# Moving V's projection ahead of the second half's queries and keys in a transformer layer on one core

## The chip, the cores and the metric

One core of a Trainium2 chip. The time is device microseconds (us) of one execution. Three runs of the kernel before gave 2120.45, 2121.21 and 2126.31 us; the median is 2121.21.

## The reference, cut to what matters

One layer of a transformer with layer norm ahead of attention and of a linear map, for 32 batches of 512 tokens with 256 channels, all float32; 16 heads of 16 channels.

```python
x = L0_attn_x                                    # 32 x 512 x 256
y = layernorm(x)
q, k, v = split_heads(y @ qkv_w.T)               # 16 heads x 16
q, k = rotate(q), rotate(k)                      # rotary positions
attn = q @ k.T * 16 ** -0.5 + alibi              # slopes * 8 * min(key - query, 0)
o = softmax(attn) @ v
x = x + o @ proj_w.T + proj_b
x = x + layernorm(x) @ (W + C @ V_r.T).T + b
```

## The kernel before, in words

Each engine's program is written out by hand, as one pass over slots (`FIRST_SLOT` to `END_SLOT`), and every slot has two halves. Slot 16 b + h does the scores of head h of batch b, so a batch is 16 slots or 32 halves; `now` (2 slot + half) counts halves. In this text half k of a batch is the half with now = 32 (b - 1) + k, from 0 to 31, while the scores of batch b - 1 are made; what is prepared in them is for batch b. Engines wait for one another by semaphores alone, and each runs its own instructions in order.

In every half TensorE (`tensor_program`) does, in this order:
- twice a score for the row maxima (`max_scores`, L428, into one of the two banks of `ps_s`) and a transposed score of the head 11 slots earlier (`exp_scores`, L438, into `ps_t`). The score waits until VectorE has read the one two before it in that bank (`max_done`); the first transposed score of a half waits for the exponential of two halves before (`exp_done`), which reads the same half of `ps_t`.
- what the tables at the top set for this half, all of it in the one bank `ps_misc`. The unit is a quarter: 4 matmuls of 32 x 256, which the trace counts as 8. A table entry (-10, (2, 2)) is: begins at half -10 (22 of the batch before), 2 quarters, then 2. `QK` has four chunks for each batch (queries and keys of heads 0 to 7, then of heads 8 to 15; `project_qk`, L396), `V` two pieces, `PROJ` and `FFN` the output maps (`linear`, L409). `XT`, `X2T` (turns), `DEN` (spread of the denominators, L470) and the row maxima (L461) have halves of their own. The first matmul of each waits until another engine has emptied the bank.
- eight matmuls (the trace's 16) of the weighted values of the head 12 slots earlier (`weighted_values`, L451, into `ps_o`). The last of a head raises `pv_done`.

VectorE reads each score with the bias and takes the row maximum (`row_maximum`, L608), adds the bias of the diagonal blocks to the transposed scores (`diagonal_bias`, L618), and at a few halves takes reciprocals of the denominators (`denominators`, L626), divides or adds. ScalarE takes one exponential a half (L794), and empties `ps_misc` where a filling ends (`empty_bank`): `raw` for queries and keys (L774), `v_one` for V (`place_v`, L750), `xt` for turns. It stands in ScalarE's order ahead of the exponential of that half. Every fourth slot, in the second half, it also copies `ps_o` to `o_sb` (L856). Means and squares of the next batches (L726, L731) stand there too. GpSimd turns `raw` (L944, L946) at the slots in `ROTATE`, and makes the high and low parts of queries and keys (L961 to L968). SP issues the DMAs.

`place_v` for batch b >= 2 has a second wait: `v_one` has two buffers, and V of batch b - 2 must have been used, which is `pv_done` at 16 (b - 1). The copy of `o_sb` waits for `pv_done` of its four heads, and half 23's copy waits for this same count:

```python
            def place_v(b, u):
                act.wait_ge(misc_full, full_at["v", b, u])
                if b >= 2:
                    act.wait_ge(pv_done, H * (b - 1))
```

The raw copy of chunk cc (`empty_bank`) waits for `rope_done` at cc, GpSimd's turn of the chunk before, since `raw` is one buffer.

Of the kernel before, what the change touches and what calls it, by code (L numbers as in the profile page):

```python
# [41 lines left out]
T_LAG, PV_LAG = 11, 12  # L42


QK = ((-24, (2, 1, 1)), (-21, (1, 1, 1, 1)), (-10, (2, 2)), (-4, (2, 1, 1)))
V = ((-8, (2, 2)), (-6, (2, 2)))
PROJ = ((66, (2, 2)), (68, (2, 2)))
FFN = ((82, (2, 2)), (84, (2, 2)))
XT, DEN, X2T = (-26, -25), (63, 64), (79, 80)

ROTATE = (-11, -9, -4, -1)
FIRST_SLOT = -21

SOONER = 8
# [57 lines left out]
def layer(nc, x, qkv_w, proj_w, proj_b, slopes, w, wb, v_r, c_r, consts, out):  # L112
    ctx = ExitStack()
    with ctx:
# [180 lines left out]
        def batch_at(slot, begin):  # L295

            b, off = divmod(slot - begin, H)
            return b if off == 0 and 0 <= b < NB else None
# [18 lines left out]
        def due(half, begin, counts=(1,)):  # L317

            for i, count in enumerate(counts):
                b, off = divmod(half - begin - i, 2 * H)  # L320
                if off == 0 and 0 <= b < NB:
                    return b, range(sum(counts[:i]), sum(counts[:i]) + count)
            return None, ()

        def complete_at(half, begin, counts=(1,)):

            b, off = divmod(half - begin - len(counts) + 1, 2 * H)
            return b if off == 0 and 0 <= b < NB else None

        def chunk_complete(half):  # L330

            for c, piece in enumerate(QK):
                b = complete_at(half, *piece)
# [4 lines left out]
        def chunk_rotated(slot):  # L338
            for c, begin in enumerate(ROTATE):
                b = batch_at(slot, begin)  # L340
                if b is not None:
                    return 4 * b + c
            return None
# [5 lines left out]
        def head_at(slot, begin):  # L349
            return slot - begin if 0 <= slot - begin < NH else None  # L350
# [12 lines left out]
        def tensor_program():  # L363
# [142 lines left out]
            for slot in range(FIRST_SLOT, END_SLOT):  # L506
# [9 lines left out]
                for half in range(2):  # L516
# [6 lines left out]
                    for u in range(2):  # L523
                        b, quarters = due(now, *V[u])
                        for quarter in quarters:
# [14 lines left out]
                    for c in range(4):  # L540
                        b, quarters = due(now, *QK[c])
                        for quarter in quarters:
# [19 lines left out]
        def vector_program():  # L562
# [25 lines left out]
            def normalise_last():  # L588

                dve.wait_ge(rstd_done2, NB)  # L590
                dve.nop(nofuse=True)
                for t in range(T):
                    ins = dve.tensor_scalar(x_hat2[:, t, :], x1[:, t, :], minus_mean[:, 1, t:t + 1],  # L593
                                            rstd[:, 1, t:t + 1], ALU.add, ALU.mult)
                ins.then_inc(xhat_done2, 1)

            def row_maximum(n, t):
                hb, hh = divmod(n, 8)
                h, k = n % H, T * n + t
                if hh == 0 and t == 0 and hb >= 2:  # L600
                    dve.wait_ge(max_split, hb - 1)
                if n < H and t == 0:
                    dve.wait_ge(alibi_done, h + 1)
                dve.wait_ge(s_done, k + 1)
                dve.nop(nofuse=True)
                off = FREE + h * N - t * P
                unused = early_junk[:, t, :] if n < T_LAG else junk[:, t % 2, :]
                dve.tensor_tensor_reduce(unused, scores_bank(n, t), alibi[:, off:off + N], 1.0, LOWEST,  # L608
                                         ALU.add, ALU.max, row_max[:, hb % 2, t, hh:hh + 1]).then_inc(max_done, 1)

            def diagonal_bias(n, pair):

                h = n % H
                dve.wait_ge(t_done, T * n + 2 * pair + 2)
                whole = ps_t[:, :, :]
                blocks = bass.AP(whole.tensor, whole.offset + 2 * pair * (N + P), [[T * N, P], [N + P, 2], [1, P]])
                table = diag[:, :].rearrange("p (o q) -> p o q", o=1).broadcast_to([P, 2, P])
                dve.scalar_tensor_tensor(out=blocks, in0=table, scalar=slope8[:, h:h + 1], in1=blocks,  # L618
                                         op0=ALU.mult, op1=ALU.add).then_inc(diag_done, 1)

            def denominators(b, half):

                if half == 0:
                    dve.wait_ge(den_placed, 16 * G * (b + 1))
                mine = slice(half * HALF, (half + 1) * HALF)
                dve.reciprocal(den[0:T * H, mine], den[0:T * H, mine]).then_inc(den_done, 1)  # L626

            def divide(b, kc):
                dve.wait_ge(misc_full, full_at["den", b, kc])
                if kc == 0:  # L630
                    dve.wait_ge(num_placed, 16 * T * G * (b + 1))
                    if b:
                        dve.wait_ge(x1_done, 2 * b)
                dve.tensor_tensor(attn_t[:, kc, :], bank_at("den", b, kc), num[:, kc, :], ALU.mult).then_inc(attn_done, 1)  # L634

            def add_linear(kind, b, u, dst, other, other_ready, done):
                dve.wait_ge(misc_full, full_at[kind, b, u])
                if u == 0:
                    dve.wait_ge(other_ready, b + 1)
                bank = bank_at(kind, b, u)  # L640
                two = slice(2 * u, 2 * u + 2)
                dve.tensor_tensor(dst[:, two, :], bank.rearrange("p (t c) -> p t c", t=2),
                                  other[:, two, :], ALU.add).then_inc(done, 1)
# [40 lines left out]
            for slot in range(FIRST_SLOT, END_SLOT):  # L684
                n, nt = head_at(slot, 0), head_at(slot, T_LAG)
                for half in range(2):
                    if n is not None:
                        row_maximum(n, 2 * half)
                        row_maximum(n, 2 * half + 1)
                    for part in range(2):  # L690
                        b = batch_at(slot, (29, 30)[part])
                        if b is not None and half == 1 - part:
                            denominators(b, part)
                    now = 2 * slot + half
                    for kc in range(KC):
                        b = complete_at(now, DEN[kc])
                        if b is not None:
                            divide(b, kc)
                    for u in range(2):
                        b = complete_at(now, *PROJ[u])  # L700
                        if b is not None:
                            add_linear("proj", b, u, x1, x_res, res_biased, x1_done)
                        b = complete_at(now, *FFN[u])
                        if b is not None:
                            add_linear("ffn", b, u, y, y, x1_biased, y_done)
                    if nt is not None:
                        diagonal_bias(nt, half)
                if slot == (NB - 1) * H + 37:
                    normalise_last()

        def scalar_program():
# [48 lines left out]
            def empty_bank(now):  # L760
# [14 lines left out]
                for u in range(2):  # L775
                    b = complete_at(now, *V[u])
                    if b is not None:
# [300 lines left out]

        tensor_program()
        vector_program()  # L1080
        scalar_program()
        pool_program()
# [30 lines left out]
```

## Time and profile before

| what | value |
|---|---|
| median of three runs | 2121.21 us |
| profiled execution, its own time | 2132.63 us |
| its span | 2131.0 us |
| mean granted clock of TensorE | 0.98 |
| TensorE busy (matmuls) | 2085.0 us, 98% |
| VectorE busy | 1892.6 us, 89% |
| ScalarE busy | 1514.3 us, 71% |
| GpSimd busy | 1301.2 us, 61% |
| one batch in the middle | 62.9 us |

The page's busy time is a union of what ran on an engine. Matmuls overlap one another in it, and their ends are modelled. The timeline is read by starts: from one first score (L428, every second one) to that of the next half is the length of a half.

### The profile page before, as it was taken

The numbers are of one execution on the slowest core, as the hardware profiler recorded it, in microseconds if no ns is written. First come the engines' busy times: TensorE is split into PE (matmuls) and PEld (weight loads), VectorE is DVE, ScalarE is ACT, GpSimd is POOL, SyncE is SP. The second block draws the span as 40 slices with busy tenths as digits, with TensorE's granted clock in tenths as the row PEclk, the third lists the DMA queues.
The fourth block names the chain that finished last, engine by engine and source line by source line (L and its number), as shares of the span: only waits on it lengthen the run. The fifth ranks groups of instructions, "written<-read, shape, count | busy, mean of one in ns | idle before, by whom it ended". The sixth has DMA issues, their size and how long they took to land.

```text
span 2131.0 us, 81880 instructions
## 1 busy us (share of the span) xinstructions
PE 2085.0 (98%) x33572; PEld 1202.0 (56%) x33572; DVE 1892.6 (89%) x5439; ACT 1514.3 (71%) x2562; POOL 1301.2 (61%) x1095
## 2 busy tenths in 40 slices
PE   5999999999999999999999999999999999999996
PEld 3455555555555555555555555555555555555553
DVE  5799999999999999999999999999999999999962
ACT  2377777777777777777777777777777777777762
POOL 6457565666666666756566666666675656666410
PEclk9799999999999999999999999999999999999996
DMA  6233333333333333333333333333433333333210
GB/s 165 82 114 102 94 112 106 103 112 111 99 106 117 93 110 117 102 94 112 107 101 112 117 95 106 115 93 108 119 102 94 112 104 104 112 106 108 87 30 26
DMA packets 158886, 218.76 MB, mean 103 GB/s; under 512 B 19024, under 2 KB 104912, under 8 KB 158512
## 3 DMA queue, kind: packets, MB, share of 16 engines
q1 hardware_dynamic: 157232, 211.44, 33.4%
q8 instruction: 264, 4.33, 0.9%
q10 hardware_dynamic: 1280, 2.10, 0.3%
q14 instruction: 110, 0.90, 0.1%
HBM read 36.52 MB, written 16.78 MB: 25 GB/s over the span
## 4 chain that ended last, share of the span: by engine, by line
PE 91%; DVE 1%; issue 1%; ACT 1%; SPq 0%; POOL 0%; DMA 0%; DVEq 0%
PE ps_s L428 29%; PE ps_o L451 21%; PE ps_misc L409 18%; PE ps_misc L396 12%; PE ps_misc L383 3%; PE ps_misc L470 3%; PE ps_t L438 3%; PE ps_misc L461 2%; DVE junk L608 1%; ACT pt L794 0%; DVE x_hat L593 0%; ACT x_hat L742 0%; DVE ps_t L618 0%; ACT x_hat L737 0%; PE ps_s L409 0%
## 5 line engine op out<-in xcount | busy, mean ns | idle before, releaser
L608 DVE CUSTOM_DVE_ANT_0 junk<-ps_s,alibi 128x512 bf16<-128x512 f32 x2004 | 1303.3, 688 | 144.3 <-PE ps_s L428 126.7
L794 ACT ACTIVATE pt<-ps_t 128x1024 f32<-128x1024 f32 x1024 | 1049.7, 1025 | 466.6 <-DVE ps_t L618 452.4
L438 PE MATMUL ps_t<-at 64*128 64x512 f32 x2048 | 763.6, 452 | 2.1 <-ACT pt L794 2.1
L428 PE MATMUL ps_s<-at 64*128 64x512 f32 x2004 | 761.7, 456 | 1.9 <-DVE row_max L608 1.3
L451 PE MATMUL ps_o<-pt,v_one 128*17 128x128 f32 x16384 | 640.8, 274 | 1.4 <-ACT pt L794 1.4
L451 PEld LDWEIGHTS ps_o<-pt,v_one 128*17 128x17 f32 x16384 | 442.2, 98 | 186.8 <-issue 45.5
L618 DVE SCALAR_TENSOR_TENSOR ps_t<-diag,slope,ps_t 128x256 f32<-128x256 f32 x1024 | 489.7, 478 | 21.1 <-PE ps_t L438 21.1
L428 PEld LDWEIGHTS ps_s<-at 64*128 64x128 f32 x2004 | 325.7, 184 | 236.5 <-DVE row_max L608 130.8
L944 POOL TENSOR_TENSOR rope_b<-raw,rope_sin 128x512 f32<-128x512 f32 x128 | 164.7, 1287 | 329.1 <-ACT raw L774 328.9
L961 POOL TENSOR_TENSOR halves<-rope_a,swapped 128x512 fp32r<-128x512 f32 x128 | 161.7, 1285 | 316.8 <-DMA swapped<-rope_b 316.8
L438 PEld LDWEIGHTS ps_t<-at 64*128 64x128 f32 x2048 | 330.3, 185 | 17.6 <-ACT pt L794 9.9
L396 PE MATMUL ps_misc<-xt,wqkv_t 128*32 128x256 f32 x4096 | 305.1, 395 | 3.5 <-DVE wqkv_t L658 2.1
L396 PEld LDWEIGHTS ps_misc<-xt,wqkv_t 128*32 128x32 f32 x4096 | 95.9, 110 | 146.5 <-issue 77.7
L608 DVE DVE_READ_ACCUMULATOR2_ANT row_max<- 128x1 f32 x2048 | 170.4, 83 | 0.0
L946 POOL TENSOR_TENSOR rope_a<-raw,rope_cos 128x512 f32<-128x512 f32 x128 | 164.9, 1288 | 0.0
L968 POOL TENSOR_TENSOR halves<-rope_a,halves 128x512 fp32r<-128x512 f32 x128 | 162.1, 1289 | 0.0
L964 POOL TENSOR_TENSOR rope_a<-rope_a,swapped 128x512 f32<-128x512 f32 x128 | 161.5, 1285 | 0.0
L409 PE MATMUL ps_misc<-wqkv_t,xt 128*32 128x256 f32 x2048 | 136.6, 385 | 1.6 <-ACT raw L774 0.9
L409 PE MATMUL ps_misc<-ffn_t,x_in 128*32 128x256 f32 x2016 | 137.3, 391 | 0.9 <-ACT x_in L717 0.8
L409 PE MATMUL ps_misc<-proj_t,attn_t 128*32 128x256 f32 x2016 | 136.4, 389 | 0.9 <-DVE attn_t L634 0.9
L883 POOL TENSOR_TENSOR x_hat<-x_hat,rstd 128x1024 f32<-128x1024 f32 x63 | 119.6, 1898 | 4.9
L774 ACT COPY raw<-ps_misc 128x512 f32<-128x512 f32 x128 | 74.6, 582 | 41.4 <-PE ps_misc L396 35.8
(94 smaller groups left out, 1712.7 us busy)
## 6 DMA issues: line engine op xcount, KB each, us to landing
at<-halves SPq DMA_DIRECT2D x192, 512.0 KB, 3.8
swapped<-rope_b SPq DMA_DIRECT2D x256, 128.0 KB, 2.6
x_in<-in_L_attn_x_dram SPq DMA_DIRECT2D x32, 512.0 KB, 5.2
num<-o_sb SPq DMA_DIRECT2D x512, 32.0 KB
x_res<-in_L_attn_x_dram SPq DMA_DIRECT2D x32, 512.0 KB, 5.3
out_dram<-x_hat SPq DMA_DIRECT2D x32, 512.0 KB, 6.0
at<-spread_den SPq DMA_DIRECT2D x60, 64.0 KB
at<-max_t ACTq DMA_DIRECT2D x128, 16.0 KB
```

The lines of the kernel that those rows point to most:

```text
L396: ins = pe.matmul(bank[q * QUARTER:(q + 1) * QUARTER, columns], wqkv_t[:, kc, col:col + QUARTER], xt[:, kc, columns], start=(kc == 0), sto ...
L409: ins = pe.matmul(bank[q * QUARTER:(q + 1) * QUARTER, part * C:(part + 1) * C], src[:, kc, tok:tok + QUARTER], weight[:, kc, :], start=(kc ...
L428: pe.matmul(scores_bank(n, t), operand(n, 0)[:, t * P:(t + 1) * P], operand(n, 1), start=True, stop=True).then_inc(s_done, 1)
L438: pe.matmul(ps_t[:, j, :], operand(n, 1)[:, j * P:(j + 1) * P], operand(n, 0), start=True, stop=True).then_inc(t_done, 1)
L451: ins = pe.matmul(ps_o[32 * t:32 * t + D + 1, hh, :], v_one[:, b % 2, j, h, :], pt[:, h % 2, j, t * P:(t + 1) * P], start=(j == 0), stop=( ...
L608: dve.tensor_tensor_reduce(unused, scores_bank(n, t), alibi[:, off:off + N], 1.0, LOWEST, ALU.add, ALU.max, row_max[:, hb % 2, t, hh:hh + ...
L618: dve.scalar_tensor_tensor(out=blocks, in0=table, scalar=slope8[:, h:h + 1], in1=blocks, op0=ALU.mult, op1=ALU.add).then_inc(diag_done, 1)
L794: act.activation(pt[:, h % 2, 2 * pair:2 * pair + 2, :], ps_t[:, 2 * pair:2 * pair + 2, :], ACT.Exp).then_inc(exp_done, 1)
L944: pool.tensor_tensor(rope_b[:, q_or_k, :], raw[:, :], rope_sin[:, :], ALU.mult) \
L946: pool.tensor_tensor(rope_a[:, q_or_k, :], raw[:, :], rope_cos[:, :], ALU.mult) \
L961: pool.tensor_tensor(halves[:, s, 0, :], rope_a[:, s, :], swapped[:, s, :], ALU.add) \
L968: pool.tensor_tensor(halves[:, s, 1, :], rope_a[:, s, :], halves[:, s, 0, :].bitcast(F32), ALU.subtract).then_inc(low_done, 1)
```

## The change

Three edits. In `QK` chunks 2 and 3 (queries and keys of heads 8 to 15) go from halves 22, 23 and 28 to 30 to halves 27, 28 and 29, 30, chunk 3 in two full halves instead of three. In `V` the two pieces go from 24, 25 and 26, 27 to 22, 23 and 24 to 26, the second with 1, 2, 1 quarters. `ROTATE` moves GpSimd's turn of chunk 2 from slot -4 to -2. And the second reciprocal (part 1) goes from the first half of its slot to the second: half 28 to 29; the first stays in 27.

```diff
-QK = ((-24, (2, 1, 1)), (-21, (1, 1, 1, 1)), (-10, (2, 2)), (-4, (2, 1, 1)))
-V = ((-8, (2, 2)), (-6, (2, 2)))
+QK = ((-24, (2, 1, 1)), (-21, (1, 1, 1, 1)), (-5, (2, 2)), (-3, (2, 2)))
+V = ((-10, (2, 2)), (-8, (1, 2, 1)))
...
-ROTATE = (-11, -9, -4, -1)
+ROTATE = (-11, -9, -2, -1)
...
                     for part in range(2):
                         b = batch_at(slot, (29, 30)[part])
-                        if b is not None and half == 1 - part:
+                        if b is not None and half == 1:
                             denominators(b, part)
```

ScalarE's order from the exponential ahead of half 23's copies (a batch in the steady part), before. `ps_misc` is the shared bank, `ps_o` the weighted values.

```order
L794 ACTIVATE pt<-ps_t 128x1024 [waits pv_done,diag_done]
L774 COPY raw<-ps_misc 128x512 [waits rope_done,misc_full]
L856 COPY o_sb<-ps_o 128x512 [waits den_placed,num_placed,pv_done]
L794 ACTIVATE pt<-ps_t 128x1024 [waits diag_done]
L794 ACTIVATE pt<-ps_t 128x1024 [waits pv_done,diag_done]
L750 COPY v_one<-ps_misc 128x32x16 [waits pv_done,misc_full]
L794 ACTIVATE pt<-ps_t 128x1024 [waits diag_done]
```

And now, from the same exponential:

```order
L794 ACTIVATE pt<-ps_t 128x1024 [waits pv_done,diag_done]
L750 COPY v_one<-ps_misc 128x32x16 [waits pv_done,misc_full]
L856 COPY o_sb<-ps_o 128x512 [waits den_placed,num_placed,pv_done]
L794 ACTIVATE pt<-ps_t 128x1024 [waits diag_done]
L794 ACTIVATE pt<-ps_t 128x1024 [waits pv_done,diag_done]
L794 ACTIVATE pt<-ps_t 128x1024 [waits diag_done]
L750 COPY v_one<-ps_misc 128x32x16 [waits pv_done,misc_full]
```

The copy of V's first piece stands where the raw copy stood, ahead of the o_sb copy and of half 23's exponential; the second piece's copy stands in half 26.

TensorE's order in half 24 and the start of half 25 of the same batch, before:

```order
L428 MATMUL ps_s<-at 128x512 [waits max_done]
L438 MATMUL ps_t<-at 128x512 [waits exp_done]
L428 MATMUL ps_s<-at 128x512 [waits max_done]
L438 MATMUL ps_t<-at 128x512
L409 MATMUL ps_misc<-wqkv_t,xt 32x256 [waits xt_done,raw_done]
L409 MATMUL ps_misc<-wqkv_t,xt 32x256 x7
L451 MATMUL ps_o<-pt,v_one 17x128 [waits exp_done,o_copied,v_staged]
L451 MATMUL ps_o<-pt,v_one 17x128 x7
L428 MATMUL ps_s<-at 128x512 [waits max_done]
L438 MATMUL ps_t<-at 128x512 [waits exp_done]
```

And now:

```order
L428 MATMUL ps_s<-at 128x512 [waits max_done]
L438 MATMUL ps_t<-at 128x512 [waits exp_done]
L428 MATMUL ps_s<-at 128x512 [waits max_done]
L438 MATMUL ps_t<-at 128x512
L409 MATMUL ps_misc<-wqkv_t,xt 32x256 [waits v_staged]
L409 MATMUL ps_misc<-wqkv_t,xt 32x256 x3
L451 MATMUL ps_o<-pt,v_one 17x128 [waits exp_done,o_copied,v_staged]
L451 MATMUL ps_o<-pt,v_one 17x128 x7
L428 MATMUL ps_s<-at 128x512 [waits max_done]
L438 MATMUL ps_t<-at 128x512 [waits exp_done]
```

Half 24 holds one quarter (4 matmuls) of V's second piece, whose first matmul waits for the copy of the first piece; before it held two quarters of the first piece, behind the raw copy.

## Rows read from the trace of the kernel before

**Rows 1.** The page, busy us (share of the span) and instructions of each engine.
```profile
PE 2085.0 (98%) x33572; PEld 1202.0 (56%) x33572; DVE 1892.6 (89%) x5439; ACT 1514.3 (71%) x2562; POOL 1301.2 (61%) x1095
```

**Rows 2.** Busy time by stretch, two batches: stretch, length, engines, clock, DMA.
```profile
961.10:1024.06 62.96, 62.96 (x1052) 36.62 (x1049) 58.36 (x169) 47.20 (x80) 40.26 (x35) 1.00 0.36 104
1024.06:1086.95 62.89, 62.89 (x1052) 36.65 (x1048) 58.31 (x169) 47.19 (x80) 41.01 (x35) 1.00 0.36 109
```

**Rows 3.** Timeline, TensorE, halves 23 to 25: start, us, what [idle before].
```profile
1024.06 0.50 PE L428 MATMUL ps_s<-at 64*128 64x512 f32 x1
...
1024.72 1.07 PE L396 MATMUL ps_misc<-xt,wqkv_t 128*32 128x256 f32 x16
1025.61 0.62 PE L451 MATMUL ps_o<-pt,v_one 128*17 128x128 f32 x16
1026.16 0.50 PE L428 MATMUL ps_s<-at 64*128 64x512 f32 x1
...
1028.26 0.50 PE L428 MATMUL ps_s<-at 64*128 64x512 f32 x1
1028.27 0.50 PE L438 MATMUL ps_t<-at 64*128 64x512 f32 x1
```

**Rows 4.** Timeline, VectorE, from half 27 to half 30.
```profile
1033.11 0.69 DVE L608 CUSTOM_DVE_ANT_0 junk<-ps_s,alibi 128x512 bf16<-128x512 f32 x1 [0.39 <-PE ps_s L428]
...
1036.44 0.54 DVE L626 RECIPROCAL den<-den 64x64 f32<-64x64 f32 x1
1036.90 0.40 DVE L618 SCALAR_TENSOR_TENSOR ps_t<-diag,slope,ps_t 128x256 f32<-128x256 f32 x1
1037.31 0.69 DVE L608 CUSTOM_DVE_ANT_0 junk<-ps_s,alibi 128x512 bf16<-128x512 f32 x1
...
1038.54 0.08 DVE L608 DVE_READ_ACCUMULATOR2_ANT row_max<- 128x1 f32 x1
```

**Rows 5.** Timeline, TensorE, first scores of halves 29 and 30.
```profile
1036.67 0.49 PE L428 MATMUL ps_s<-at 64*128 64x512 f32 x1
...
1038.34 0.49 PE L428 MATMUL ps_s<-at 64*128 64x512 f32 x1
```

**Rows 6.** Timeline, TensorE, starts of half 31 and half 32.
```profile
1040.12 0.50 PE L428 MATMUL ps_s<-at 64*128 64x512 f32 x1
1040.21 0.50 PE L438 MATMUL ps_t<-at 64*128 64x512 f32 x1
...
1042.32 0.50 PE L428 MATMUL ps_s<-at 64*128 64x512 f32 x1
```

**Rows 7.** Timeline, ScalarE, what half 23 gives it to do.
```profile
1025.86 0.58 ACT L774 COPY raw<-ps_misc 128x512 f32<-128x512 f32 x1 [0.38 <-PE ps_misc L396]
1026.34 0.59 ACT L856 COPY o_sb<-ps_o 128x512 f32<-128x512 f32 x1
1026.82 1.05 ACT L794 ACTIVATE pt<-ps_t 128x1024 f32<-128x1024 f32 x1
```

**Rows 8.** Line L750, v_one's copy: what ended the idle time before (us, times).
```profile
  PE ps_misc L409: 34.3, 64
```

**Rows 9.** Timeline, ScalarE, the o_sb copy of half 31.
```profile
1042.45 0.59 ACT L856 COPY o_sb<-ps_o 128x512 f32<-128x512 f32 x1 [0.41 <-PE ps_o L451]
```

**Rows 10.** Timeline, ScalarE, mean, squares and exponential of half 29.
```profile
1038.26 0.40 ACT L726 ACTIVATE x_hat<-x_in 128x256 f32<-128x256 f32 x1
...
1038.65 0.50 ACT L731 ACTIVATE x_hat<-x_in,minus_mean 128x256 f32<-128x256 f32 x1
...
1039.15 1.01 ACT L794 ACTIVATE pt<-ps_t 128x1024 f32<-128x1024 f32 x1
```

**Rows 11.** Timeline, GpSimd, turn of chunk 3 behind the raw copy.
```profile
1040.71 1.29 POOL L944 TENSOR_TENSOR rope_b<-raw,rope_sin 128x512 f32<-128x512 f32 x1 [8.61 <-ACT raw L774]
1041.95 1.28 POOL L946 TENSOR_TENSOR rope_a<-raw,rope_cos 128x512 f32<-128x512 f32 x1
```

**Rows 12.** Who waited for whom, TensorE: us in total, times, longest.
```profile
PE ps_t L428 <- DMA at<-halves: 5.7, 1, 5.7
```

## The prediction

> **What bounds the kernel now.** First the page's busy shares [rows 1]: TensorE has work 98% of the span, VectorE 89%, ScalarE 71%, GpSimd 61%. A share is an average, so next two whole batches [rows 2]: 62.96 and 62.89 us, TensorE busy all the time at a granted clock of 1.00. A batch is 32 half-slots; I number them 0 to 31 (half 23 starts at 1024.06 here) and read TensorE's own timeline for those that the change touches. Halves 23, 24 and 25 start at 1024.06, 1026.16 and 1028.26, each 2.10 us after the last [rows 3]: the two pairs of score and transposed score take 0.66 us, two quarters of projection 0.89, the weighted values 0.55, and the next half begins at once. In a half of that kind TensorE is the bound: VectorE stands 0.39 us idle in each until TensorE's next score is there [rows 4]. Half 29, with one quarter, takes 1038.34 - 1036.67 = 1.67 us, half 30, with one too, 1040.12 - 1038.34 = 1.78 [rows 5]: after a short half VectorE's second maximum is read only 0.3 us into the next (half 29's at 1038.54 + 0.08, for a half that starts at 1038.34 [rows 4, 5]), the second score waits for its bank, and 0.1 us goes. Half 31 takes 2.20, of which 0.09 is the wait of its first transposed score (1040.12 against 1040.21 [rows 6]) for an exponential.
>
> ScalarE is off that path but for one link: the first transposed score of half k overwrites what the exponential of half k-2 reads. Its idle time is slack only as long as that exponential ends in time. In half 23 it copies raw at 1025.86, o_sb at 1026.34 and starts the exponential at 1026.82, which ends at 1027.87 [rows 7]; half 25 needs it at 1028.27 [rows 3]. The slack is 0.40 us.
>
> **The change, part by part.**
>
> *Work.* Nothing is added or taken away: as many matmuls, copies, additions and reciprocals; SP's queue keeps its order. Quarters only change halves. Halves 22 to 30 now hold 2,2,2,2,2,2,2,1,1 quarters and get 2,2,1,2,1,2,2,2,2.
>
> *Pace, if nothing waited.* Counted from half 23's start to half 32's, before: 1042.32 - 1024.06 = 18.26 us [rows 3, 6]. After: half 23 2.10; half 24, short after a full one, 1.67; half 25, full after a short one, 2.10 + 0.10 = 2.20; half 26 1.67; half 27 2.20; halves 28 and 29 4.20; half 30 2.10 and about 0.05 for an exponential that is late there (below); half 31 no longer follows a short half and loses its 0.09: 2.11. Sum 18.30. So the two short halves, set apart, bring nothing: +0.04 us a batch. Bounds: if the 0.10 is not paid twice, -0.16; if half 31 keeps its wait, +0.13.
>
> *V's copy moves two halves forward, and its wait with it.* This is the costly part. The copy of V's first piece now stands in half 23, where it also waits for pv_done at 16(b-1). The matmul that gives this count is the last of half 23's weighted values, behind V's own last quarter in TensorE's order. Before, the copy ran two halves later and the count had long been there (its idle time was for its own fill, "PE ps_misc L409" [rows 8]). What ScalarE sees of such a release is shown one place on: the o_sb copy of half 31 starts at 1042.45, 0.13 us after half 32's first score at 1042.32 [rows 6, 9]. With half 23's start as zero: half 24 starts at 2.10, v_one is copied from 2.23; the o_sb copy behind it comes 0.48 later (spacing of the two copies, 1025.86 to 1026.34) at 2.71, the exponential another 0.48 later at 3.19 and ends at 4.24 (its 1.05 [rows 7]). A transposed score follows the end of its exponential by 0.05 (ACT 1039.15 + 1.01 = 1040.16, PE 1040.21 [rows 6, 10]). So half 25's comes at 4.29.
> Without this it would come at 2.10 + 1.67 = 3.77, and with the 0.10 that a half after a short one loses anyway its work runs as from 3.87. The wait costs 4.29 - 3.87 = 0.42 us. Behind it in TensorE's queue stand its second score, the second quarter pair of V, the weighted values and all of the next half, so it isn't made up: the halves after it are full ones.
> On the way lie two smaller waits that this one swallows: V's second piece can start in the bank when the copy has landed, at 2.23 + 0.59 + 0.05 = 2.87 instead of 2.10 + 0.66 = 2.76, and the weighted values of half 24 need o_sb copied, at 2.71 + 0.59 + 0.05 = 3.35 instead of 2.87 + 0.45 = 3.32. They make half 24 end at 3.35 + 0.55 = 3.90; the wait for the exponential lasts till 4.29.
>
> *Queries and keys two halves later.* The raw copy of chunk 2 runs in half 28 at +1.80 (as in half 23: 1025.86 - 1024.06), GpSimd turns it in 2.5 us (1.24 to the second turn, which takes 1.28 [rows 11]) and is done 0.8 us into half 30; the raw copy of chunk 3 needs it 1.8 us into half 30. Hidden, with a slack of 1.0 us, by GpSimd's 8.61 us of idle time there [rows 11]; if that cover were gone, half 31 would be late by what is missing. On ScalarE half 28 now holds raw copy (0.48), squares (0.50), mean (0.39) ahead of its exponential [rows 7, 10]: it runs from half 28's start + 1.80 + 1.37 = 3.17 to 4.19, and half 30's transposed score, due at 4.20, comes at 4.24: 0.04, taken as 0.05. Half 26's copy comes 1.80 - 0.43 = 1.37 us into that half and stands ahead of two means: its exponential runs from 1.37 + 0.48 + 0.39 + 0.39 = 2.63 to 3.66, and half 28 starts 1.67 + 2.20 = 3.87 after half 26. Nothing, with 0.15 us to spare.
>
> *Reciprocals.* The first stays in half 27, the second goes from 28 to 29. Each puts the diagonal addition off by 0.46 us, from 1036.44 to 1036.90 [rows 4]. Half 29 is now full, with 0.39 us of VectorE's slack, as 28 was; the maximum behind it still comes 0.64 us into its half, as elsewhere (1037.31, in a half that starts at 1036.67 [rows 4, 5]). The exponential of half 29 waits for mean and squares till then anyway. Cost 0, bounds 0 and 0.1. The spread of the denominators in half 31 has its reciprocals over 2 us before.
>
> *Start and end.* The first score waits for a DMA of the first half's rows with TensorE idle 5.7 us [rows 12]; V ahead of chunk 2 there fits into that wait. The copy's wait exists for batches 2 to 31 only. Both 0, bounds -0.5 and +1 us in all.
>
> **Sum.** 0.04 + 0.42 = 0.46 us in each of 30 batches: 13.8 us. The profiled execution took 2132.6 us and would take 2146.4; the median of the runs is 2121.2, 11.4 below it, so the same addition gives **2135.0 us**. Of it 0.3% or 6.4 us is what a measurement can tell from no change.
>
> **Two readings of "busy".** The page gives TensorE's weight loads 56% and its matmuls 98% [rows 1]. In a full half each group of matmuls starts when the one before has run out, and each half right behind the last [rows 3], so I count every delay in full. The Trainium skill, in "Perfetto Trace Analysis", section "Identifying the Most-Contended Engine", says that matmul busy time is a poor measure for TensorE, and to judge its headroom by flops and the share of weight-load time. By that TensorE would have 44% to spare and VectorE be the engine that decides; it is rival 2. The sum by it would be near 0.
>
> **Rivals.**
> 1. *Faster: short halves pay and the wait is hidden.* It needs ScalarE to see pv_done 0.5 us sooner than at half 32 [rows 9], or half 25 to start later than its exponential. Then, with the 0.10 not paid again either, -0.16 to -0.20 a batch: 2116 us. Against it: the matmul that releases the copy stands last in half 23. 0.04.
> 2. *No change: the wait falls into slack.* TensorE waits, but the halves behind are VectorE's to pace. Then +0.04 a batch, 2122.4 us. For it: VectorE at 89%. Against: 0.39 us of VectorE idle in each full half behind it [rows 4]. 0.09.
> 3. *Slower by more: the waits add.* Each of the three waits in halves 24 and 25 exposes a weight load and another at half 30 grows, or half 28's exponential is late too, since half 26's copy stands ahead of the means: +0.7 to +0.9 a batch, 2142 to 2148 us. It decides if ScalarE loses 0.15 us more than I count. 0.15.
> 4. *The change doesn't do this*, since the copy's count is one that was reached a slot earlier. The order of instructions speaks against: the o_sb copy beside it waits for the same count, and ran right then. Price as rival 2; inside its chance.
>
> **Numbers.** My case: 0.72, with 2129 to 2141 for +0.27 to +0.65 a batch. Taking in part of rival 3 the range is 2128 to 2143. Faster by over 0.3%: 0.04; within: 0.09 and a little of my own case's lower end, 0.11; slower: 0.85.
>
> **What would show it.** Halves 24 and 25 together take 4.2 to 4.3 us, with TensorE's first transposed score of half 25 about 0.4 us behind its score, waiting for ScalarE; the v_one copies show 30 waits for ps_o L451; the copy starts 0.13 us into half 24; a batch takes about 63.4 us. Halves 26 at 1.67, 27 at 2.20, 31 at 2.11. It is wrong if the copy in half 23 starts before half 24, if half 25's transposed score follows its score at once, or if a batch stays at 62.9.

## The result and the profile after

The changed kernel took 2144.04 us (median of 4 runs, 2140.27 to 2151.85), the kernel before beside it 2123.03 us (4 runs, 2120.45 to 2126.31). The ratio is 1.0099, with a 95% interval of 1.0079 to 1.0120: slower by 17 to 25 us. It was forecast slower, at 2135.0 us with a range up to 2143.0. The direction held, the size didn't: the time lies 1 us above the range and 9 us above the forecast. One execution of experiment 2, 7592.52 us against 2126 to 2142 us of its nine others, is left out of that experiment's ratio; nothing here explains it.

The page of the changed kernel: its span, busy us of each engine, and the chain that ended last by line:

```profile
span 2138.9 us, 81880 instructions
PE 2088.6 (98%) x33572; PEld 1195.3 (56%) x33572; DVE 1891.5 (88%) x5439; ACT 1513.8 (71%) x2562; POOL 1302.5 (61%) x1095
...
PE ps_s L428 28%; PE ps_o L451 21%; PE ps_misc L409 18%; PE ps_misc L396 12%; PE ps_t L438 3%; PE ps_misc L383 3%; PE ps_misc L470 3%; PE ps_misc L461 2%; ACT v_one L750 1%; DVE junk L608 1%; ACT pt L794 0%; DVE x_hat L593 0%; ACT x_hat L742 0%; DVE ps_t L618 0%; ACT x_hat L737 0%
```

The shares are those of [rows 1] but for VectorE's, 88% where it was 89%, so they alone would not tell the kernels apart. One entry is new: the copy to v_one (L750) is in the chain that ended last, with 1% of the span. The span of this profiled execution is only 7.9 us longer than before's. To see why, the span has to be cut where batches begin: start to batch 1, batches 1 to 30, and the rest. The columns are stretch, length, busy us of PE, PEld, DVE, ACT and POOL, granted clock, DMA share, GB/s. The kernel before:

```profile
0.00:102.38 102.38, 78.42 (x652) 38.98 (x653) 67.05 (x195) 30.64 (x76) 57.74 (x52) 0.80 0.45 128
102.38:1987.77 1885.39, 1884.47 (x31272) 1095.02 (x31272) 1745.75 (x5037) 1408.96 (x2367) 1210.78 (x1017) 1.00 0.36 106
1987.77:2130.96 143.19, 122.11 (x1652) 68.01 (x1648) 79.80 (x209) 74.70 (x120) 32.70 (x28) 0.85 0.14 43
```

The changed kernel, cut at the same places of the program:

```profile
0.00:104.34 104.34, 79.58 (x652) 39.29 (x653) 67.14 (x195) 30.61 (x76) 58.06 (x52) 0.79 0.44 125
104.34:2007.34 1903.00, 1898.68 (x31273) 1092.76 (x31273) 1744.56 (x5037) 1408.73 (x2367) 1211.87 (x1017) 1.00 0.35 105
2007.34:2138.90 131.56, 110.38 (x1652) 63.29 (x1648) 79.82 (x209) 74.46 (x120) 32.56 (x28) 0.94 0.16 47
```

The 30 batches took 17.6 us more, 0.59 each on average (batch 1 took 0.84 more, those behind it 0.58), at a granted clock of 1.00 in both. The end took 11.6 us less, with the same instructions on TensorE: its granted clock was 0.94 there instead of 0.85. That is a matter of the single execution, as the experiments show, so I compare the middle stretch from here on.

TensorE's timeline for halves 24 and 25 of the same batch as in [rows 3] (half 23 starts at 1034.55):

```profile
1036.65 0.50 PE L428 MATMUL ps_s<-at 64*128 64x512 f32 x1
...
1037.48 0.64 PE L409 MATMUL ps_misc<-wqkv_t,xt 128*32 128x256 f32 x8
1038.02 0.63 PE L451 MATMUL ps_o<-pt,v_one 128*17 128x128 f32 x16
1038.58 0.50 PE L428 MATMUL ps_s<-at 64*128 64x512 f32 x1
1038.90 0.50 PE L438 MATMUL ps_t<-at 64*128 64x512 f32 x1
...
1040.99 0.50 PE L428 MATMUL ps_s<-at 64*128 64x512 f32 x1
```

And ScalarE's, which answers to [rows 7]:

```profile
1036.84 0.59 ACT L750 COPY v_one<-ps_misc 128x512 f32<-128x512 f32 x1 [0.87 <-PE ps_o L451]
1037.32 0.59 ACT L856 COPY o_sb<-ps_o 128x512 f32<-128x512 f32 x1
1037.80 1.04 ACT L794 ACTIVATE pt<-ps_t 128x1024 f32<-128x1024 f32 x1
```

ScalarE stood 0.87 us idle for the weighted values, copied V at 0.19 us into half 24, o_sb at 0.67, and its exponential ended at 1037.80 + 1.04 = 1038.84. Half 25's first score had been started at 1038.58, its transposed score had to wait till 1038.90. The forecast had this at 4.29 us after half 23's start; it came at 1038.90 - 1034.55 = 4.35. Of the 64 copies of V, 30 waited for the weighted values and 33 for their own filling (where [rows 8] have 64 that waited for their own filling):

```profile
  PE ps_o L451: 26.7, 30
  PE ps_misc L409: 18.3, 33
```

The lengths of the halves, medians over 28 batches, in ns (a sum is the sum of two medians):

| half | before | after | forecast |
|---|---|---|---|
| 22, 23 | 2101, 2102 | 2101, 2102 | 2100 each |
| 24 + 25 | 4203 | 4344 | 4290 |
| 26, 27 | 2101, 2103 | 1669, 2204 | 1670, 2200 |
| 28, 29 | 2101, 1667 | 2100, 2101 | 2100 each |
| 30 | 1777 | 2144 | 2150 |
| 31 | 2204 | 2112 | 2110 |
| 34 (2 of the next batch) | 2338 | 2391 | 2338 |
| whole batch, mean | 62988 | 63565 | +460 |

(The forecast for 24 + 25 is 4.29 - 2.10 to the transposed score, and 2.10 from there.) Two lines are off: 24 + 25 by 0.05 us, and half 34, of which the forecast said nothing, by 0.05.

### The profile page after: what moved, and what is told of

The parts are those of the page before. It is cut to its first block, busy times and chain, and to the rows that moved or that the text cites. A ratio compares the mean times of both kernels' runs of the same rounds, so it can differ in the third digit from the quotient of the medians.

```text
span 2138.9 us, 81880 instructions
## 1 busy us (share of the span) xinstructions
PE 2088.6 (98%) x33572; PEld 1195.3 (56%) x33572; DVE 1891.5 (88%) x5439; ACT 1513.8 (71%) x2562; POOL 1302.5 (61%) x1095
## 4 chain that ended last, share of the span: by engine, by line
PE 90%; DVE 1%; ACT 1%; issue 1%; SPq 0%; POOL 0%; ACTq 0%; DMA 0%; DVEq 0%
PE ps_s L428 28%; PE ps_o L451 21%; PE ps_misc L409 18%; PE ps_misc L396 12%; PE ps_t L438 3%; PE ps_misc L383 3%; PE ps_misc L470 3%; PE ps_misc L461 2%; ACT v_one L750 1%; DVE junk L608 1%; ACT pt L794 0%; DVE x_hat L593 0%; ACT x_hat L742 0%; DVE ps_t L618 0%; ACT x_hat L737 0%
## 5 line engine op out<-in xcount | busy, mean ns | idle before, releaser
L451 PE MATMUL ps_o<-pt,v_one 128*17 128x128 f32 x16384 | 637.8, 273 | 1.4 <-ACT pt L794 1.4
L451 PEld LDWEIGHTS ps_o<-pt,v_one 128*17 128x17 f32 x16384 | 438.9, 97 | 189.1 <-issue 56.4
L396 PE MATMUL ps_misc<-xt,wqkv_t 128*32 128x256 f32 x4096 | 297.8, 393 | 4.2 <-DVE wqkv_t L658 2.1
L409 PE MATMUL ps_misc<-wqkv_t,xt 128*32 128x256 f32 x2048 | 144.6, 390 | 4.2 <-ACT v_one L750 1.2
```

The source lines that it names most:

```text
L396: ins = pe.matmul(bank[q * QUARTER:(q + 1) * QUARTER, columns], wqkv_t[:, kc, col:col + QUARTER], xt[:, kc, columns], start=(kc == 0), sto ...
L409: ins = pe.matmul(bank[q * QUARTER:(q + 1) * QUARTER, part * C:(part + 1) * C], src[:, kc, tok:tok + QUARTER], weight[:, kc, :], start=(kc ...
L451: ins = pe.matmul(ps_o[32 * t:32 * t + D + 1, hh, :], v_one[:, b % 2, j, h, :], pt[:, h % 2, j, t * P:(t + 1) * P], start=(j == 0), stop=( ...
```

## The experiments

There are ten more runs: eight variants, and both kernels once more. Each is judged by its middle stretch, batches 1 to 30, which two profiles of one kernel repeat to 0.13 us. "A batch" is the mean over 28 batches, as in the table. Where no ratio to before is given, a variant was run once. The expectations were on record before.

### 1. The wait taken away (e1_three_buffers)

V's first piece gets three buffers, so that its copy waits for the weighted values of a batch earlier.

```diff
-        v_one = sb("v_one", [P, 2, T, H, D + 1])
+        v_one = [sb("v_one_a", [P, 3, 2, H, D + 1]), sb("v_one_b", [P, 2, 2, H, D + 1])]
...
-                if b >= 2:
-                    act.wait_ge(pv_done, H * (b - 1))
+                if b >= 3 - u:
+                    act.wait_ge(pv_done, H * (b - 2 + u))
...
```

> The changed kernel, but V's first piece has three buffers instead of two, so that its copy in half 23 waits for weighted values that were done a batch earlier; nothing else differs. Theory (the copy's wait for the last weighted value of half 23 delays the exponential that half 25 needs): the copy starts 1.80 us into half 23, halves 24 and 25 take 1.67 + 2.20 = 3.87 us instead of 4.34, a batch falls from 63.56 to about 63.09 us and the time by some 14 us against the change. Rival (the costly part is the spread of the quarters over halves, or the queries' and keys' later place): halves 24 and 25 and the batch stay as in the change.

Measured: the middle stretch took 1889.43 us, 13.6 less than the change's 1903.00, a batch 63.11. Timed: 1.0022 of before (1.0001 to 1.0044). Half 23 starts at 1027.43 in this profile. What half 23 gives ScalarE to do:

```profile
1029.23 0.59 ACT L750 COPY v_one_a<-ps_misc 128x512 f32<-128x512 f32 x1 [0.38 <-PE ps_misc L409]
1029.71 0.59 ACT L856 COPY o_sb<-ps_o 128x512 f32<-128x512 f32 x1
1030.19 1.04 ACT L794 ACTIVATE pt<-ps_t 128x1024 f32<-128x1024 f32 x1
```

TensorE, the first scores of halves 24, 25 and 26:

```profile
1029.53 0.50 PE L428 MATMUL ps_s<-at 64*128 64x512 f32 x1
...
1031.20 0.50 PE L428 MATMUL ps_s<-at 64*128 64x512 f32 x1
1031.29 0.50 PE L438 MATMUL ps_t<-at 64*128 64x512 f32 x1
...
1033.40 0.49 PE L428 MATMUL ps_s<-at 64*128 64x512 f32 x1
```

The copy starts 1.80 us into half 23 and now waits for its own filling; half 24 takes 1.67, half 25 2.20. Both halves are as the theory had them, and the rival, by which they would have stayed as in the change, is out. The wait for the weighted values costs 13.6 us of the 17.6. What is left, 1889.43 - 1885.39 = 4.0 us, is the rest of the change (experiment 3 takes it up). (The transposed score of half 25 is 0.09 us late even here, since the exponential ends at 1031.23; it falls into the 0.10 that a half behind a short one loses anyway.)

### 2. V ahead, but its copy a half later (e3_first_piece_spread)

```diff
-V = ((-10, (2, 2)), (-8, (1, 2, 1)))
+V = ((-10, (1, 2, 1)), (-7, (2, 2)))
```

> The changed kernel with V's first piece over three halves (22 to 24, 1, 2 and 1 quarters) and its second in two full ones (25, 26); so V still stands ahead of the second half's queries and keys, but its first copy falls into half 24, where the count it waits for is there. Theory (only the wait in half 23 costs): halves 22 to 31 sum to 20.4 us (20.37 before, 20.89 in the change), a batch takes 63.0 to 63.1 us, the time is 2 to 4 us above before. Rival (the order V, then queries and keys, costs by itself, on GpSimd or ScalarE): a batch of 63.4 us or more.

Measured: middle stretch 1893.92 us, a batch 63.28: 9.1 us better than the change, but above the 63.0 to 63.1 expected. Timed: 1.0034 of before (1.0009 to 1.0059), 7 us where 2 to 4 were expected, with an interval from 2 to 13. The order of V and keys is cleared, since the rival wanted 63.4 or more. The surplus sits in one half: half 23 took 2.40 us, not 2.20. VectorE, ScalarE and TensorE around it (half 22 starts at 1022.79, half 23 at 1024.46):

```profile
1022.56 0.69 DVE L642 TENSOR_TENSOR x_hat<-ps_misc,x_hat 128x512 f32<-128x512 f32 x1
...
1023.16 0.48 DVE L618 SCALAR_TENSOR_TENSOR ps_t<-diag,slope,ps_t 128x256 f32<-128x256 f32 x1
...
1023.68 1.02 ACT L794 ACTIVATE pt<-ps_t 128x1024 f32<-128x1024 f32 x1 [1.56 <-DVE ps_t L618]
1024.46 0.50 PE L428 MATMUL ps_s<-at 64*128 64x512 f32 x1
1024.76 0.50 PE L438 MATMUL ps_t<-at 64*128 64x512 f32 x1
```

The addition of half 21 (L642) stands ahead of that half's diagonal addition, the exponential comes late, ends at 1024.70, and half 23's transposed score has to wait 0.30 us. It is the same link as in the change, fed from VectorE this time. In the kernel before the same exponential ended 0.19 us ahead of half 23 (1022.84 + 1.03 = 1023.87 against 1024.06), since a full half 22 gave 0.43 us more. In this kernel a half can be made short without loss only where the exponential of the half before it is early.

### 3. The spread alone (e4_no_reorder)

```diff
-QK = ((-24, (2, 1, 1)), (-21, (1, 1, 1, 1)), (-5, (2, 2)), (-3, (2, 2)))
-V = ((-10, (2, 2)), (-8, (1, 2, 1)))
+QK = ((-24, (2, 1, 1)), (-21, (1, 1, 1, 1)), (-10, (2, 2)), (-3, (2, 2)))
+V = ((-8, (2, 2)), (-6, (1, 2, 1)))
...
-ROTATE = (-11, -9, -2, -1)
+ROTATE = (-11, -9, -4, -1)
```

> Only the spread: chunk 2 of queries and keys and V's first piece stay in halves 22 to 25 as before, V's second piece takes halves 26 to 28 (1, 2, 1), chunk 3 halves 29 and 30 in full, reciprocals as in the change. Theory (short halves set apart bring nothing and cost nothing): halves 26 and 28 take 1.67, halves 27 and 29 2.20, half 31 2.11, half 34 2.39 instead of 2.34; a batch 63.0 us, the time within 2 us of before. Rival (the spread is what costs the change its time): a batch above 63.3 us.

Measured: middle stretch 1889.50 us, 4.1 above before and the same as experiment 1; a batch 63.12, 0.12 above the 63.0 expected. Halves 26 to 29 took 1669, 2204, 1668 and 2216 ns, half 31 2111, half 34 2392. Timed: 1.0020 of before (0.9994 to 1.0047), 4 us where 2 at most were expected, which doesn't tell it from before; the stretch does. So the spread costs 0.13 us a batch (63.12 - 62.99), not 0.04. In the halves that the sum covers it is nearly as forecast: medians of halves 22 to 31 add up to 20409 ns in experiment 1 against 20359 before, +0.05. Of the rest 0.05 us lie in half 34, and some 0.02 in a few ns each in halves further on, which I can't trace. In this experiment chunk 2 and its turn on GpSimd stand where they were before, in experiment 1 five halves and two slots later; both take the same time, so their move costs nothing that shows.

Half 34 is explained by the traces. VectorE from half 31 to half 33 in the kernel before (half 31 starts at 1040.12, half 34 at 1046.19), then the exponential of half 32 and the transposed score of half 34 behind it:

```profile
1040.76 0.69 DVE L608 CUSTOM_DVE_ANT_0 junk<-ps_s,alibi 128x512 bf16<-128x512 f32 x1
...
1044.23 0.69 DVE L634 TENSOR_TENSOR attn_t<-ps_misc,num 128x512 f32<-128x512 f32 x1
1044.84 0.48 DVE L618 SCALAR_TENSOR_TENSOR ps_t<-diag,slope,ps_t 128x256 f32<-128x256 f32 x1
...
1045.35 1.02 ACT L794 ACTIVATE pt<-ps_t 128x1024 f32<-128x1024 f32 x1 [1.19 <-DVE ps_t L618]
...
1046.43 0.50 PE L438 MATMUL ps_t<-at 64*128 64x512 f32 x1
```

In the changed kernel (half 31 starts at 1051.22, half 34 at 1057.20):

```profile
1051.86 0.69 DVE L608 CUSTOM_DVE_ANT_0 junk<-ps_s,alibi 128x512 bf16<-128x512 f32 x1 [0.43 <-PE ps_s L428]
...
1055.30 0.68 DVE L634 TENSOR_TENSOR attn_t<-ps_misc,num 128x512 f32<-128x512 f32 x1
1055.91 0.48 DVE L618 SCALAR_TENSOR_TENSOR ps_t<-diag,slope,ps_t 128x256 f32<-128x256 f32 x1
...
1056.42 1.02 ACT L794 ACTIVATE pt<-ps_t 128x1024 f32<-128x1024 f32 x1 [1.19 <-DVE ps_t L618]
...
1057.50 0.50 PE L438 MATMUL ps_t<-at 64*128 64x512 f32 x1
```

In both kernels VectorE's first maximum of half 31 starts 0.64 us into the half, when its score is there. From there four maxima, two divisions and the diagonal addition of half 31 stand one behind the other up to that of half 32, at 1044.84 - 1040.12 = 4.72 and 1055.91 - 1051.22 = 4.69 us into half 31. Half 31 got 0.09 us shorter on TensorE, VectorE's chain only 0.03. The exponential of half 32 waits for that chain, and half 34's transposed score for the exponential: it came 0.24 us behind half 34's start before and 0.30 in the change. Of the 0.09 gained at half 31, 0.05 was given back three halves on.

### 4. The second reciprocal alone, in the kernel before (e2_reciprocals_only)

```diff
-                        if b is not None and half == 1 - part:
+                        if b is not None and half == 1:
```

> The kernel before with the second reciprocal moved from half 28 to half 29, and nothing else. In this table half 29 is short. Theory (VectorE has 0.39 us to spare in a full half and none in a short one): VectorE ends half 29 0.46 us late, halves 30 and 31 together take 0.3 to 0.4 us more, a batch about 63.3 us. Rival (the reciprocal is off every path that counts): a batch of 62.99 us.

Measured: middle stretch 1894.31 us, 8.9 above before; a batch 63.28, half 31 2511 ns instead of 2204. VectorE behind half 29's second maximum (the half starts at 1042.74), and TensorE at half 31's start:

```profile
1044.61 0.54 DVE L626 RECIPROCAL den<-den 64x64 f32<-64x64 f32 x1
1045.08 0.40 DVE L618 SCALAR_TENSOR_TENSOR ps_t<-diag,slope,ps_t 128x256 f32<-128x256 f32 x1
```

```profile
1046.18 0.49 PE L428 MATMUL ps_s<-at 64*128 64x512 f32 x1
1046.59 0.50 PE L438 MATMUL ps_t<-at 64*128 64x512 f32 x1
```

The theory holds. The exponential of half 29 waited for the diagonal addition behind the reciprocal, started at 1045.51 and ended at 1046.53, and half 31's transposed score came 0.41 us behind its score instead of 0.09: 0.46 us of VectorE in a short half cost 0.30 us of the batch. This edit would have been a loss alone; in the change it costs nothing because half 29 is full there.

### 5. The second reciprocal back, in the changed kernel (e9_second_reciprocal_back)

```diff
-                        if b is not None and half == 1:
+                        if b is not None and half == 1 - part:
```

> The changed kernel with the second reciprocal back in half 28, which is full in the new table, as half 29 is. Theory (a reciprocal is free in any full half): a batch 63.56 us, halves 28 to 31 as in the change. Rival (half 29 was the better place): half 30 or 31 changes by 0.1 us or more.

Measured: middle stretch 1902.84 us against 1903.00 and 1903.06, halves 28 to 31 2099, 2104, 2146 and 2110 ns. No difference. In a full half the reciprocal is free, in either.

### 6 and 7. One more copy in half 23, before and after (e5_more_copy_before, e6_more_copy_after)

```diff
-        x_res = sb("x_res", [P, T, C])
+        x_res, scratch = sb("x_res", [P, T, C]), sb("scratch", [P, 512])
...
+                    if slot % H == 11:
+                        act.copy(scratch[:, :], ps_o[:, :, :].rearrange("p a b -> p (a b)"))
                     act.copy(o_sb[:, :, :], ps_o[:, :, :]).then_inc(o_copied, 1)
```

> The kernel before with one copy more on ScalarE in half 23, ahead of the o_sb copy: ps_o to a buffer that nobody reads, 0.48 us of ScalarE's time. Theory (the exponential of half 23 has 0.40 us of slack there, less 0.05 for its release): 0.13 us a batch are lost, in half 24 or 25, the rest of the copy falls into the slack; a batch 63.1 us. Rival (ScalarE is off the path): 62.99 us.

> The changed kernel with the same additional copy in half 23. Theory (the chain from the last weighted value of half 23 over the copies and the exponential to half 25's transposed score is the path): all of the 0.48 us is lost, a batch 64.04 us instead of 63.56, halves 24 and 25 together 4.83 us. Rival (the change's loss lies elsewhere): the loss is as in the kernel before, some 0.1 us a batch.

In the kernel before: middle stretch 1889.54, 4.2 us more, 0.14 a batch (63.12). In the changed kernel: 1917.55, 14.5 us more than the change, 0.48 a batch (64.05); halves 24 and 25 together 4.83 us. ScalarE and TensorE in the first, where half 25 starts at 1027.95:

```profile
1026.98 1.06 ACT L794 ACTIVATE pt<-ps_t 128x1024 f32<-128x1024 f32 x1
```

```profile
1027.95 0.50 PE L428 MATMUL ps_s<-at 64*128 64x512 f32 x1
1028.09 0.49 PE L438 MATMUL ps_t<-at 64*128 64x512 f32 x1
```

The exponential ends at 1028.04, and the transposed score follows 0.05 later, 0.14 behind its score. The same copy costs 0.14 us where the exponential had 0.35 us of room (the 0.40 read in half 23 less 0.05 for the release of the transposed score) and all of its 0.48 where the room was used up. Both are as expected to 0.02 us, so that reading was right, and the path of the changed kernel runs through ScalarE's copies.

### 8. The order of the two waits (e7_waits_swapped)

```diff
-                act.wait_ge(misc_full, full_at["v", b, u])
                 if b >= 2:
                     act.wait_ge(pv_done, H * (b - 1))
+                act.wait_ge(misc_full, full_at["v", b, u])
```

> The changed kernel with the two waits ahead of the copy of V in the other order: first for the weighted values, then for the bank. In the change the copy starts 0.19 us into half 24, the o_sb copy of half 31 0.14 us into half 32 after the same kind of release. Theory (the wait that stands last and is released last costs 0.055 us more): the copy starts at 0.14, a batch falls by 0.05 us to 63.51. Rival (it is the copy or its place that is slower): 0.19 and 63.56 as before.

Measured: middle stretch 1901.35, 1.65 us less; a batch 63.51. The copy of half 23, with half 24's start at 1034.54:

```profile
1034.67 0.59 ACT L750 COPY v_one<-ps_misc 128x512 f32<-128x512 f32 x1 [0.81 <-PE ps_o L451]
```

It starts 0.14 us into the half instead of 0.19. That the one that comes last stood last in the program's order of two waits cost 0.055 us a batch here (1.65 / 30).

### 9 and 10. Both kernels again (e8_change_again, e10_before_again)

> The changed kernel once more, unaltered, beside more runs of the kernel before: how much of the first comparison's 21 us is the steady part (0.577 us in 30 batches, 17.3 us) and how much the start and the end of single runs. Theory (the steady part is nearly all): 17 to 19 us above before. Rival (the start costs 1 us and the end some more in every run): 21 us or more.

> The kernel before once more, for a second profile. Theory (the batches in the middle repeat, the start and the end of the program don't): 62.99 us a batch; the part from the last score to the end differs from 86.5 us of the first profile by some us, by TensorE's granted clock. Rival (each kernel has its own end): 86.5 us again.

The change again: 2145.12 us (median of 4) against 2124.91 (7 runs of before), ratio 1.0090 (1.0054 to 1.0125). 20 us, above the 17 to 19 of the theory, with an interval that holds both and the rival. The profiles tell more. The change:

```profile
0.00:98.68 98.68, 73.36 (x653) 37.24 (x653) 66.85 (x195) 30.63 (x76) 58.01 (x52) 0.83 0.46 132
98.68:2001.74 1903.06, 1898.76 (x31274) 1092.80 (x31274) 1744.89 (x5037) 1409.46 (x2367) 1212.96 (x1017) 1.00 0.35 105
2001.74:2145.30 143.56, 122.45 (x1652) 67.98 (x1648) 79.83 (x209) 74.79 (x120) 32.57 (x28) 0.85 0.14 43
```

And the kernel before:

```profile
0.00:103.28 103.28, 79.69 (x652) 38.96 (x653) 69.21 (x195) 30.55 (x76) 57.76 (x52) 0.77 0.44 127
103.28:1988.54 1885.26, 1884.37 (x31273) 1094.25 (x31273) 1745.23 (x5037) 1409.19 (x2367) 1210.68 (x1017) 1.00 0.36 106
1988.54:2122.90 134.36, 113.26 (x1652) 64.26 (x1648) 79.80 (x209) 74.50 (x120) 32.71 (x28) 0.92 0.15 46
```

The middle repeats (1903.06 and 1903.00, 1885.26 and 1885.39). The end took 143.19 and 134.36 us in two executions of the kernel before, 131.56 and 143.56 in two of the changed one: the longer the lower the granted clock, whichever kernel. From the last score to the end alone, the 86.5 us of the last expectation were 77.7 this time. The start varied too, from 98.7 us at a granted clock of 0.83 to 104.3 at 0.79, both in the changed kernel. Neither goes with the kernel.

## Why the prediction was wrong in size and right in direction

**Right: the mechanism.** "V's copy moves two halves forward, and its wait with it" is the change's loss. The link from the last weighted value over two copies and the exponential to half 25's transposed score is shown by its removal (experiment 1: -13.6 us), by a copy added to it (+0.48 us a batch in experiment 7, +0.14 in 6, as worked out from the slack), and by the 30 copies that wait for L451. The forecast lengths of halves 26, 27, 28 to 30 and 31 stand within 0.01 us. The cause I gave is thus shown; what failed are sizes of terms and the base they were added to.

**Right: what costs nothing.** The reciprocal (experiment 5) and GpSimd's later turn of chunk 2: the turn ended 0.79 us into half 30, the raw copy of chunk 3 started 1.84 us into it, and half 30 was as forecast. My reason for the reciprocal, that a full half has the slack for it, is shown by experiments 4 and 5 together: it costs 0.30 us in a short half and nothing in either full one.

**Mis-sized: the release of the copy.** I took 0.13 us after half 24's start, from the o_sb copy of [rows 9]; it was 0.19. The difference is the order of the two waits (experiment 8) and makes 1.65 us in all. The wait as a whole cost 13.6 us or 0.45 a batch (experiment 1), where the sum had 0.42.

**Mis-sized: "half 31 no longer follows a short half and loses its 0.09".** It did, but I ended the sum at half 32. VectorE's chain of divisions gave 0.05 us of it back in half 34, 1.6 us in all. This term of the sum should have been followed until a half that waits for nobody. With what stayed untraced in experiment 3, the spread costs 0.13 us a batch and not 0.04, as the sum had it.

**The base.** The sum gave 13.8 us for what was 17.6 in the middle stretch, 3.8 short; the two terms above make 3.3 of it. The other 5.2 of the miss of 9.0 us lie outside the middle stretch: the median that I added the sum to, 2121.2 of three runs, was low. Over the 25 runs beside experiments 1 to 4 the kernel before had a median of 2125.8, and 2125.8 + 17.6 = 2143.4 is 0.6 from what the changed kernel took. This is argued from the spread of the runs, not shown run by run: the 21.0 us between the two medians of the first comparison are 3.4 more than the middle stretch explains, and start and end, which varied by up to 5.7 and 12.0 us within one kernel, can hold that. The measured loss of 0.58 us a batch lies within the bounds of my own case, +0.27 to +0.65; the time fell out of the range by way of the base.

**The rivals.** Rival 2, that VectorE paces the halves and the wait falls into slack, is refuted by experiments 1 and 7: nothing of 0.48 us was absorbed. With it goes the reading that the Trainium skill ("Perfetto Trace Analysis", section "Identifying the Most-Contended Engine") would suggest by its share of weight-load time: weight loads were busy 56% of the span, before and after, and TensorE still made up nothing of a delay in the full halves behind it. The page's other measure, flops against the peak, was not worked out. Rivals 1 and 4 are out by the copy's start, 0.19 us into half 24, and by the 30 copies that waited for L451. Rival 3, waits that add, didn't occur. Its price, 2142 to 2148 us, holds the measured time, but that is chance: its mechanism asked for 0.7 to 0.9 us a batch, 0.58 were measured, and the low base made up the rest. The smaller waits in half 24 were swallowed, as said: half 24 took 1.93 us where I had 3.90 - 2.10 = 1.80, and the wait for the exponential still decided when half 25's work began, so that its transposed score stood 0.32 us behind its score and not 0.39.

None of the variants beats the kernel before; the nearest, experiments 1 and 3, lose 4 us in the middle stretch.

## What to carry to other kernels

Where an engine runs a fixed order, read for each step that is moved what else it waits for at its new place, and from where in the order of the other engine that comes: a count that was reached long before can be the last thing to arrive two places earlier. The slack of an engine off the path is that of one link in one stage, here 0.35 us on an engine that is 29% idle. And follow a gain or loss past the last edited place, until nothing waits for what it moved.

## What the runs showed of the hardware

Two waits ahead of one ScalarE instruction cost 0.055 us more when the semaphore that comes last is the one that the program waits for last (copy at 0.19 us against 0.14 into the half, experiment 8). And the last 130 to 145 us of the program, in which TensorE stands idle for 21, took up to 12 us more or less at a mean granted clock of 0.85 to 0.94, in executions of the same kernel. The ten us that begin 30 us behind the last score ran at a granted clock of 0.50, the lower level of 1.2 GHz, in the first profile of the kernel before and at 1.00 in the first of the changed one. It had begun to fall in the ten us ahead of these (0.69 against 1.00), and in the ten before those TensorE was busy for 9.05 us in both, so what decides it is not shown. The 12 us are two thirds of what the change cost, and medians of three or four runs tell such a change less well than one stretch of a profile.
